# Order of the bf16 and the fp32 products inside the row-tiled fills of a three-layer decoder kernel

## Chip, cores and metric

The kernel runs on one core of one Trainium2 chip. The metric is the device time of one execution in microseconds; for the kernel before it is 3608.37 us, the median of three runs (3608.07 to 3608.52).

## What is computed

The input is x, 64 sequences of 256 tokens with 256 features, and a context of 64 x 120 x 256. Every sequence passes, on its own, through four blocks, each with a layer norm ahead and a residual sum behind:

```python
x = x + local_attention(ln(x))          # 16 heads of 16, each token sees 7 neighbours
x = x + cross_attention(ln(x), ctx)     # 16 heads, 256 queries, 120 keys
x = x + causal_attention(rms(ln(x)))    # 16 heads, 256 queries, 256 keys, mask above the diagonal
x = x + gated_mlp(rms(ln(x)))           # 256 -> 1024 -> 256, weighted by a top-2 gate
```

The change touches only the scores of the cross and the causal attention. They are computed twice. A first time (step "max") with the queries on the partitions, to find each query's maximum m over the keys of each head; a second time (step "scores") with the keys on the partitions, to form exp(scale * (k.q - m)), which is then multiplied with the values.

## The kernel before

**Steps and order.** A planner (class Plan) simulates the engines with written costs and writes out one fixed order of steps for each engine; five sequences are in flight at a time, so neighbouring steps on TensorE mostly belong to different sequences. A step of TensorE waits on semaphores for its operands and for PSUM banks to be emptied, issues its products, and signals the banks as filled (`filled[b]`); ScalarE or VectorE read the bank and signal `emptied[b]`. The costs of the planner are not touched by the change, so the order of steps on every engine stays.

**Row-tiled fills.** A head has 16 features, and two heads share 32 partitions, so the products of "max" (line 756) and "scores" (line 788) contract over 32 rows only. They use the array as four row groups, r = 0 to 3 (`tile_position=(32 * r, 0)`), each writing its own PSUM bank: a fill takes four banks at once. Four products, one in each row group, run beside one another; they are called a quad here. Each fp32 product of the source is two instructions on the chip, each with a weight load of its own; a bf16 product is one. All other steps (projections, transposes, MLP, values) use the array in another shape.

**What is added in bf16.** In the causal "max" fills the mask is added by small bf16 products, `pick_rows` times `mask_rows` (line 750), that add -1e30 above the diagonal. In all "scores" fills the negated maxima are added by `pick` times `nmaxT` (line 780). Before the change these stand first in their fill, with `start=True` on the first of a bank, and the fp32 products accumulate on top. Cross "max" fills have no bf16 part.

**Fills of one sequence,** with quads as instructions on the chip:

| fill | bf16 quads (columns) | fp32 quads (columns) |
|---|---|---|
| cross max, two of them | none | 8 (120) |
| cross scores, two | 2 (256), weights 32x120 | 4 (256) |
| causal max, block 0 | 4 (128) | 8 (128) |
| causal max, block 1, two | 4 (64) | 4 (256) |
| causal scores, units 0 and 1 | 2 (256) | 4 (256) |
| causal scores, unit 2 | 4 (128) | 8 (128) |

**Order around them.** In the trace the steps of TensorE come back in one cyclic order, about 55 us a round, and the ten fills stand in six groups: (a) behind transposes (680): causal scores unit 2, then cross max, then a projection (722); (b) behind that projection: cross max, then causal max block 0, then transposes (687); (c) behind transposes: cross scores, then a projection (700); (d) behind a projection (839): cross scores, then a causal max of block 1, then 700; (e) behind transposes: the other causal max of block 1, then the values (811); (f) behind an MLP product (860): causal scores unit 0, then unit 1, then the MLP's second product (869). Causal scores unit 1 needs a bank that VectorE empties at line 1355.

Of the kernel before, what the change touches and what calls it, by code (L numbers as in the profile page):

```python
# [7 lines left out]
P = 128  # L8
# [10 lines left out]
SLOT = 32  # L19
# [15 lines left out]
LOCAL, CROSS, CAUSAL = 0, 1, 2  # L35
# [6 lines left out]
HEADS = [(m, e, r) for m in range(2) for e in range(2) for r in range(4)]  # L42
# [9 lines left out]
def key_blocks(layer, T, C):  # L52

    if layer == CROSS:
        return [(0, C, 0, T, 0)]
    return [(0, P, 0, T, 0), (P, P, P, P, T)]
# [344 lines left out]
def decoder(nc, t, out):  # L401
    B, T, D = t["x"].shape
    C = t["ctx_1024"].shape[1]
# [6 lines left out]
    with ExitStack() as ctx:  # L410
# [6 lines left out]
        ps = ctx.enter_context(nc.psum_tensor("ps", [P, 8, 512], F32))  # L417
# [15 lines left out]
        pick = sb("pick", [P, 4, P], BF16)  # L433
# [8 lines left out]
        pick_rows = sb("pick_rows", [P, 4, P], BF16)  # L442
# [9 lines left out]
        qT = [[held[s][:, 2 + 2 * e:4 + 2 * e, :] for e in range(2)] for s in range(LANES)]  # L452
        kT = [held[s][:, 6:8, :] for s in range(LANES)]
# [16 lines left out]
        nmaxT = per_lane("nmaxT", [P, T], BF16)  # L470
# [8 lines left out]
        ms = per_lane("ms", [P, 2])  # L479
# [33 lines left out]
        filled = [sem(f"filled{b}") for b in range(BANKS)]  # L513
# [57 lines left out]
        with nc.Block(no_gpsimd_drain=True) as block:  # L571
# [71 lines left out]
            def _(pe):  # L643
# [15 lines left out]
                for name, seq, args in plan.order["PE"]:  # L659
                    s = plan.lane[seq]  # L660
                    once(pe, known, "constants", constants, 16)
                    if name == "derive":

                        b = bank(name, seq, (0,))
                        for slab in range(4):
                            last = nc.tensor.matmul(ps[:, b, slab * P:(slab + 1) * P], like_rows[:, slab, :],
                                                    ident_b[:], start=(slab == 0), stop=(slab == 3),
                                                    skip_group_check=True)
# [3 lines left out]
                                         stop=True).then_inc(filled[b], 1)  # L672
                    elif name == "turn":
# [3 lines left out]
                        for k in range(2):  # L677
                            for tb in range(2):
                                col = k * T + tb * P
                                last = nc.tensor.transpose(ps[:, b, col:col + P], xn[s][:, tb, k * P:(k + 1) * P],  # L680
                                                           ident[:])
                        last.then_inc(filled[b], 1)
                    elif name == "turn_ctx":
                        pe.wait_ge(ctx_loaded[s], reached["ctx_loaded", "load", seq, ()])
                        b = bank(name, seq, args)
                        for k in range(2):
                            last = nc.tensor.transpose(ps[:, b, k * C:(k + 1) * C], cx[s][0:C, k * P:(k + 1) * P],
                                                       ident[0:C, 0:C])
                        last.then_inc(filled[b], 1)
                    elif name == "project_rows":  # L690
                        w, = args
                        n = 1 if w == "q" else 0
# [3 lines left out]
                        for tb in range(2):  # L696
                            for k in range(2):

                                tokens = xT[s][:, k, :].rearrange("p (t b) -> p b t", b=2)[:, tb, :]
                                last = nc.tensor.matmul(ps[:, b, tb * D:(tb + 1) * D], tokens,  # L700
                                                        W[f"local_{w}"][:, k, :], start=(k == 0), stop=(k == 1))
                        last.then_inc(filled[b], 1)
                    elif name == "project":
                        L, w = args
# [6 lines left out]
                        if L == CROSS and w != "q":  # L711
                            wait_taken(pe, "turn_ctx", seq)
                            src, n = cT[s], C
                        else:
                            wait_taken(pe, "turn", seq, L)
                            src, n = xT[s], T
                        b = bank(name, seq, args)
                        wt = W[f"{NAMES[L]}_{w}"]
                        if w in "qk":
                            for m in range(2):  # L720
                                for k in range(2):
                                    last = nc.tensor.matmul(ps[:, b, m * n:(m + 1) * n], wt[:, k, m * P:(m + 1) * P],  # L722
                                                            src[:, k, 0:n], start=(k == 0), stop=(k == 1))
                        else:
                            for tb in range((n + P - 1) // P):
                                rows = min(P, n - tb * P)
                                for k in range(2):
                                    last = nc.tensor.matmul(ps[0:rows, b, tb * D:(tb + 1) * D],  # L728
                                                            src[:, k, tb * P:tb * P + rows], wt[:, k, :],
                                                            start=(k == 0), stop=(k == 1))  # L730
                        last.then_inc(filled[b], 1)
                    elif name == "max":
                        L, f = args
                        tb, ms, keys = max_fills(L, T, C)[f]
# [5 lines left out]
                            wait_taken(pe, "project", seq, L, w)  # L740
                        to = banks(name, seq, args)
                        count = 2 * len(ms)
                        if L == CAUSAL:

                            for slab in range(4):
                                for r in range(4):
                                    rows = slice(32 * r, 32 * r + 32)
                                    of_heads = ps[:, to[r], 0:count * keys].rearrange("p (g k) -> p g k", k=keys)
                                    first = tb * P + SLOT * slab
                                    nc.tensor.matmul(of_heads[:, :, first:first + SLOT], pick_rows[rows, slab, :],  # L750
                                                     mask_rows[rows, :].unsqueeze(1).to_broadcast([32, count, SLOT]),
                                                     start=(slab == 0), stop=False, tile_position=(32 * r, 0),
                                                     skip_group_check=True)
                        for n, (m, e, r) in enumerate((m, e, r) for m, e, r in HEADS if m in ms):
                            rows, place = slice(32 * r, 32 * r + 32), n // 4
                            last = nc.tensor.matmul(ps[:, to[r], place * keys:(place + 1) * keys],  # L756
                                                    qT[s][e][rows, m, tb * P:(tb + 1) * P], kT[s][rows, m, 0:keys],
                                                    start=(L == CROSS and place == 0), stop=True,
                                                    tile_position=(32 * r, 0), skip_group_check=True)
                            if place == count - 1:  # L760
                                last.then_inc(filled[to[r]], 1)
                    elif name == "shift":
                        L, = args
                        pe.wait_ge(nmax_ready[s], reached["nmax_ready", "round_max", seq, (L,)])
                        b = bank(name, seq, args)
                        to = ps[:, b, :].bitcast(BF16)
                        for tb in range(2):
                            last = nc.tensor.transpose(to[:, tb * P:(tb + 1) * P], nmax_parts[s][:, tb, :],
                                                       ident_b[:])
                        last.then_inc(filled[b], 1)  # L770
                    elif name == "scores":
                        L, u = args
                        once(pe, known, "pick", derived["pick"], 1)
                        wait_taken(pe, "shift", seq, L)
                        to, unit = banks(name, seq, args), score_units(L)[u]
                        for n, (g, kb) in enumerate(unit):
                            key0, keys, q0, qs, col = key_blocks(L, T, C)[kb]
                            for r in range(4):
                                rows = slice(32 * r, 32 * r + 32)
                                nc.tensor.matmul(ps[0:keys, to[r], n * qs:(n + 1) * qs], pick[rows, g, 0:keys],  # L780
                                                 nmaxT[s][rows, q0:q0 + qs], start=(n == 0), stop=False,
                                                 tile_position=(32 * r, 0), skip_group_check=True)
                        for n, (g, kb) in enumerate(unit):
                            m, e = divmod(g, 2)
                            key0, keys, q0, qs, col = key_blocks(L, T, C)[kb]
                            for r in range(4):
                                rows = slice(32 * r, 32 * r + 32)
                                last = nc.tensor.matmul(ps[0:keys, to[r], n * qs:(n + 1) * qs],  # L788
                                                        kT[s][rows, m, key0:key0 + keys],
                                                        qT[s][e][rows, m, q0:q0 + qs], start=False, stop=True,  # L790
                                                        tile_position=(32 * r, 0), skip_group_check=True)
                                if n == len(unit) - 1:
                                    last.then_inc(filled[to[r]], 1)
                    elif name == "values":
                        L, = args
# [7 lines left out]
                        for m in range(2):  # L803
                            b = bank(name, seq, (L, m))
                            for e in range(2):
                                g = 2 * m + e
                                pr = prob_of(seq, L, g)
                                for kb, (key0, keys, q0, qs, col) in enumerate(blocks):
                                    for j in range(4):
                                        head = VW * (8 * m + 2 * j + e)  # L810
                                        last = nc.tensor.matmul(ps[SLOT * j:SLOT * (j + 1), b, e * T + q0:e * T + q0 + qs],  # L811
                                                                va[s][0:keys, kb, head:head + SLOT],
                                                                pr[0:keys, j, col:col + qs],
                                                                start=(e == 0 and kb == 0),
                                                                stop=(kb == len(blocks) - 1),
                                                                tile_position=(0, SLOT * j), skip_group_check=True)
                            last.then_inc(filled[b], 1)
                    elif name == "turn_out":
# [3 lines left out]
                        for k in range(2):  # L822
                            for tb in range(2):
                                col = k * T + tb * P
# [3 lines left out]
                    elif name == "project_out":  # L828
                        L, = args
# [13 lines left out]
                    elif name == "gate":  # L843
# [3 lines left out]
                        for tb in range(2):  # L847
                            for k in range(2):
                                last = nc.tensor.matmul(ps[:, b, tb * E:(tb + 1) * E],  # L849
                                                        xT[s][:, k, tb * P:(tb + 1) * P], w_gate[:, k, :],  # L850
                                                        start=(k == 0), stop=(k == 1))
# [557 lines left out]
```

## Time and profile before

| | |
|---|---|
| median of three runs | 3608.37 us |
| the profiled execution: its own time | 3603.33 us |
| its span, first to last instruction | 3601.5 us |
| PE busy | 3488.3 us, 97% |
| PEld (weight loads) busy | 2853.8 us, 79% |
| DVE, POOL, ACT busy | 77%, 70%, 48% |
| PE's share of the chain that ended last | 93% |

PE is the row of matrix products, PEld that of the weight loads of the same engine, which overlap it. A timeline row gives the start of a block of equal instructions in us from the start of the span, the length of the block from its first start to its last end, and how many instructions were merged; a product's recorded end is later than the end of its stream of columns by a constant, so the lengths of two blocks of one shape are compared, or starts with starts.

### The profile page before, as it was taken

What the parts mean: (1) busy time and instruction counts of PE and PEld (TensorE: products, weight loads), DVE (VectorE), ACT (ScalarE), POOL (GpSimd) and SP (SyncE); (2) the same over time, 40 slices, a digit from 0 to 9 for tenths busy, and PEclk for the clock granted to TensorE, in tenths of its full rate; (3) what the DMA queues carried; (4) which work ended last, traced back from release to release, by engine and by line L of the source; (5) the groups of instructions that cost most, each with busy time, mean ns of one, the idle gap of its engine ahead of it and who ended that gap; (6) DMA issues with size and microseconds to landing.
All of it is one profiled execution on the core that took longest, in us unless ns stands there. A gap on an engine that the chain in (4) does not pass through costs nothing.

```text
span 3601.5 us, 97036 instructions
## 1 busy us (share of the span) xinstructions
PE 3488.3 (97%) x38789; PEld 2853.8 (79%) x38789; DVE 2764.0 (77%) x6256; ACT 1715.7 (48%) x4049; POOL 2507.6 (70%) x3159
## 2 busy tenths in 40 slices
PE   6699999999999999999999999999999999999998
PEld 5578888888888888888888888888888888888876
DVE  5677787787787787787787877877877877877863
ACT  2345545545545445445545545445445455455443
POOL 5767777777777677677677777777677677677742
PEclk8899999999999999999999999999999999999999
DMA  5111111111121121121121121111111111111100
GB/s 177 48 50 59 61 67 53 66 69 48 67 72 45 67 74 45 67 74 45 67 74 45 67 73 46 67 67 53 67 63 57 67 60 60 67 57 62 67 8 10
DMA packets 87098, 221.54 MB, mean 62 GB/s; under 512 B 8262, under 2 KB 53634, under 8 KB 70274
## 3 DMA queue, kind: packets, MB, share of 16 engines
q1 hardware_dynamic: 86658, 215.34, 16.9%
q8 instruction: 317, 5.19, 0.6%
q14 instruction: 123, 1.01, 0.1%
HBM read 164.92 MB, written 50.39 MB: 60 GB/s over the span
## 4 chain that ended last, share of the span: by engine, by line
PE 93%; DVE 4%; ACT 2%; issue 1%; POOL 0%; DMA 0%; SPq 0%; DVEq 0%; ACTq 0%
PE ps L869 13%; PE ps L860 13%; PE ps L722 11%; PE ps L700 10%; PE ps L839 9%; PE ps L756 8%; PE ps L811 8%; PE ps L788 6%; PE ps L728 5%; PE ps L680 3%; PE ps L780 3%; PE ps L849 2%; DVE held L1355 1%; PE ps L750 1%; ACT rest L1002 1%; DVE nmax_pair L1292 1%
## 5 line engine op out<-in xcount | busy, mean ns | idle before, releaser
L1124 POOL TENSOR_TENSOR chunks<-v_windows,xT 128x560 f32<-128x560 f32 (+1 forms) x384 | 870.8, 2284 | 259.0 <-DVE xT L1267 155.0
L1292 DVE TENSOR_REDUCE nmax_pair<-ps 128x4 f32<-128x480 f32 (+2 forms) x1280 | 776.1, 669 | 167.8 <-PE ps L756 167.5
L1119 POOL TENSOR_TENSOR chunks<-rest,k_windows 128x512 f32<-128x512 f32 (+1 forms) x384 | 552.9, 1455 | 436.8 <-DVE xT L1246 232.6
L969 ACT ACTIVATE prob<-ps 128x256 f32<-128x256 f32 (+2 forms) x1536 | 670.0, 548 | 331.9 <-PE ps L788 331.9
L860 PE MATMUL ps<-xT,w_up 128*128 128x256 f32 x2048 | 483.7, 384 | 0.0
L869 PE MATMUL ps<-w_down,held 128*128 128x256 f32 x2048 | 458.9, 382 | 1.8 <-DVE held L1355 1.6
L869 PEld LDWEIGHTS ps<-w_down,held 128*128 128x128 f32 x2048 | 383.9, 190 | 72.2 <-issue 20.4
L860 PEld LDWEIGHTS ps<-xT,w_up 128*128 128x128 f32 x2048 | 375.7, 191 | 44.7 <-issue 0.9
L1246 DVE TENSOR_REDUCE xT<-chunks 128x32 f32<-128x512 f32 (+1 forms) x384 | 294.0, 766 | 128.0 <-POOL chunks L1119 128.0
L927 ACT COPY xT<-ps 128x512 f32<-128x512 f32 x256 | 149.8, 585 | 489.3 <-PE ps L680 489.2
L1136 POOL TENSOR_SCALAR_AFFINE_SELECT prob<-prob 128x512 f32<-128x512 f32 x512 | 319.5, 655 | 75.7 <-ACT prob L969 75.7
L756 PE MATMUL ps<-held 32*128 32x256 f32 (+2 forms) x8192 | 358.9, 307 | 3.4 <-ACT held L944 3.3
L788 PE MATMUL ps<-held 32*120 32x256 f32 (+2 forms) x6144 | 341.7, 345 | 0.0
L811 PE MATMUL ps<-prob,va 120*32 120x256 f32 (+2 forms) x6144 | 304.8, 346 | 3.3 <-ACT prob L969 2.4
L756 PEld LDWEIGHTS ps<-held 32*128 32x128 f32 x8192 | 280.2, 187 | 30.4 <-ACT held L940 19.6
L1246 DVE TENSOR_REDUCE held<-chunks 128x80 f32<-128x560 f32 (+1 forms) x384 | 286.8, 760 | 11.6 <-POOL chunks L1124 11.5
L1355 DVE SCALAR_TENSOR_TENSOR held<-rest,ps 128x512 f32<-128x512 f32 x256 | 175.2, 685 | 120.6 <-ACT rest L1002 120.5
L811 PEld LDWEIGHTS ps<-prob,va 120*32 120x32 f32 (+1 forms) x6144 | 180.2, 110 | 108.2 <-issue 25.8
L1002 ACT ACTIVATE rest<-ps 128x512 f32<-128x512 f32 x256 | 152.6, 597 | 224.4 <-PE ps L860 224.4
L788 PEld LDWEIGHTS ps<-held 32*120 32x120 f32 (+1 forms) x6144 | 244.5, 185 | 11.3
L915 ACT ACTIVATE held<-x,nmean,rstd 128x256 f32<-128x256 f32 x256 | 139.9, 594 | 236.5 <-POOL nmean L1072 236.5
L944 ACT ACTIVATE held<-ps,b_cross_q,half 128x256 f32<-128x256 f32 x256 | 123.5, 562 | 109.3 <-PE ps L722 109.3
(146 smaller groups left out, 6086.6 us busy)
## 6 DMA issues: line engine op xcount, KB each, us to landing
k_windows<-passed_on SPq DMA_DIRECT2D x64, 1024.0 KB, 4.6
v_windows<-passed_on SPq DMA_DIRECT2D x64, 1024.0 KB, 5.1
x<-in_x SPq DMA_DIRECT2D x64, 256.0 KB, 2.9
passed_on<-rest SPq DMA_DIRECT2D x64, 256.0 KB, 2.0
passed_on<-held SPq DMA_DIRECT2D x64, 256.0 KB, 2.0
out<-x SPq DMA_DIRECT2D x64, 256.0 KB, 2.1
y<-in_ctx SPq DMA_DIRECT2D x64, 120.0 KB, 2.8
w_up<-in_up SPq DMA_DIRECT2D x1, 1024.0 KB, 8.8
```

The lines of the kernel that those rows point to most:

```text
L700: last = nc.tensor.matmul(ps[:, b, tb * D:(tb + 1) * D], tokens, W[f"local_{w}"][:, k, :], start=(k == 0), stop=(k == 1))
L722: last = nc.tensor.matmul(ps[:, b, m * n:(m + 1) * n], wt[:, k, m * P:(m + 1) * P], src[:, k, 0:n], start=(k == 0), stop=(k == 1))
L756: last = nc.tensor.matmul(ps[:, to[r], place * keys:(place + 1) * keys], qT[s][e][rows, m, tb * P:(tb + 1) * P], kT[s][rows, m, 0:keys], s ...
L788: last = nc.tensor.matmul(ps[0:keys, to[r], n * qs:(n + 1) * qs], kT[s][rows, m, key0:key0 + keys], qT[s][e][rows, m, q0:q0 + qs], start=F ...
L811: last = nc.tensor.matmul(ps[SLOT * j:SLOT * (j + 1), b, e * T + q0:e * T + q0 + qs], va[s][0:keys, kb, head:head + SLOT], pr[0:keys, j, c ...
L860: last = nc.tensor.matmul(ps[:, b, m * T:(m + 1) * T], w_up[:, k, (2 * m2 + m) * P:(2 * m2 + m + 1) * P], xT[s][:, k, :], start=(k == 0), ...
L869: last = nc.tensor.matmul(ps[:, b, tb * D:(tb + 1) * D], hid[s][:, m, tb * P:(tb + 1) * P], w_down[:, m, :], start=(m == 0), stop=(m == F ...
L969: last = nc.scalar.activation(prob_pair(seq, L, m)[0:keys, :, r, col:col + qs], of_pair, ACT.Exp, scale=SCALE)
L1119: last = nc.gpsimd.tensor_tensor(chunk_of(c).rearrange("p (j d) -> p j d", d=D), q_row, window("k", (b + first) * D, (D, n), (1, D)), ALU. ...
L1124: last = nc.gpsimd.tensor_tensor(chunk_of(c).rearrange("p (h i j) -> p h i j", i=HD, j=WINDOW), window("v", b * D + first * HD, (HD, n), ( ...
L1246: nc.vector.tensor_reduce(to, chunk_of(c).rearrange("p (x i) -> p x i", i=width), AX_X, ALU.add).then_inc(reduced[s], 1)
L1292: nc.vector.tensor_reduce(nmax[s][:, tb, heads], src, AX_X, ALU.max, negate=True).then_inc(emptied[b], 1)
```

## The change

In both kinds of step the bf16 products move behind the fp32 ones. The fp32 product that comes first in a bank now has `start=True`; the last bf16 product of a bank now signals `filled`. Nothing is added or removed, and waits stand where they stood, at the head of the step.

```diff
@@ step "max"
                         count = 2 * len(ms)
+                        for n, (m, e, r) in enumerate((m, e, r) for m, e, r in HEADS if m in ms):
+                            rows, place = slice(32 * r, 32 * r + 32), n // 4
+                            last = nc.tensor.matmul(ps[:, to[r], place * keys:(place + 1) * keys],
+                                                    qT[s][e][rows, m, tb * P:(tb + 1) * P], kT[s][rows, m, 0:keys],
+                                                    start=(place == 0), stop=(L == CROSS),
+                                                    tile_position=(32 * r, 0), skip_group_check=True)
+                            if L == CROSS and place == count - 1:
+                                last.then_inc(filled[to[r]], 1)
                         if L == CAUSAL:
...
-                                    nc.tensor.matmul(of_heads[:, :, first:first + SLOT], pick_rows[rows, slab, :],
+                                    last = nc.tensor.matmul(of_heads[:, :, first:first + SLOT], pick_rows[rows, slab, :],
                                                      mask_rows[rows, :].unsqueeze(1).to_broadcast([32, count, SLOT]),
-                                                     start=(slab == 0), stop=False, tile_position=(32 * r, 0),
+                                                     start=False, stop=(slab == 3), tile_position=(32 * r, 0),
                                                      skip_group_check=True)
-                        for n, (m, e, r) in enumerate((m, e, r) for m, e, r in HEADS if m in ms):
-                            rows, place = slice(32 * r, 32 * r + 32), n // 4
...
+                                    if slab == 3:
+                                        last.then_inc(filled[to[r]], 1)
@@ step "scores"
                         for n, (g, kb) in enumerate(unit):
-                            key0, keys, q0, qs, col = key_blocks(L, T, C)[kb]
-                            for r in range(4):
-                                rows = slice(32 * r, 32 * r + 32)
-                                nc.tensor.matmul(ps[0:keys, to[r], n * qs:(n + 1) * qs], pick[rows, g, 0:keys],
-                                                 nmaxT[s][rows, q0:q0 + qs], start=(n == 0), stop=False,
-                                                 tile_position=(32 * r, 0), skip_group_check=True)
-                        for n, (g, kb) in enumerate(unit):
                             m, e = divmod(g, 2)
...
                                                         kT[s][rows, m, key0:key0 + keys],
-                                                        qT[s][e][rows, m, q0:q0 + qs], start=False, stop=True,
+                                                        qT[s][e][rows, m, q0:q0 + qs], start=(n == 0), stop=False,
                                                         tile_position=(32 * r, 0), skip_group_check=True)
+                        for n, (g, kb) in enumerate(unit):
+                            key0, keys, q0, qs, col = key_blocks(L, T, C)[kb]
+                            for r in range(4):
+                                rows = slice(32 * r, 32 * r + 32)
+                                last = nc.tensor.matmul(ps[0:keys, to[r], n * qs:(n + 1) * qs], pick[rows, g, 0:keys],
+                                                 nmaxT[s][rows, q0:q0 + qs], start=False, stop=True,
+                                                 tile_position=(32 * r, 0), skip_group_check=True)
                                 if n == len(unit) - 1:
                                     last.then_inc(filled[to[r]], 1)
```

## Rows read from the trace of the kernel before

**Rows 1.** The page: busy time of each engine, and the chain that ended last
```profile
PE 3488.3 (97%) x38789; PEld 2853.8 (79%) x38789; DVE 2764.0 (77%) x6256; ACT 1715.7 (48%) x4049; POOL 2507.6 (70%) x3159
...
PE 93%; DVE 4%; ACT 2%; issue 1%; POOL 0%; DMA 0%; SPq 0%; DVEq 0%; ACTq 0%
```
**Rows 2.** Waits of PE: who was waited for, total us, times, longest
```profile
PE ps L780 <- DVE held L1355: 22.5, 60, 0.4
PE ps L825 <- DVE held L1246: 16.1, 2, 15.4
```
**Rows 3.** Groups of PE by form: busy us, mean ns of one
```profile
L756 PE MATMUL ps<-held 32*128 32x120 f32 x4096 | 143.8, 278 | 3.4 <-ACT held L944 3.3
L756 PE MATMUL ps<-held 32*128 32x256 f32 x2048 | 142.8, 395 | 0.0
...
L788 PE MATMUL ps<-held 32*128 32x256 f32 x2048 | 134.5, 378 | 0.0
...
L780 PE MATMUL ps<-nmaxT,pick 32*128 32x128 bf16 x1024 | 25.7, 217 | 2.6 <-ACT prob L969 2.6
```
**Rows 4.** Timeline of PE, 1802 to 1811 us: start, length, count (groups a, b)
```profile
1802.82 0.40 PE L780 MATMUL ps<-nmaxT,pick 32*128 32x128 bf16 x16
1803.05 1.12 PE L788 MATMUL ps<-held 32*128 32x128 f32 x32
1804.00 1.05 PE L756 MATMUL ps<-held 32*128 32x120 f32 x32
...
1808.64 1.17 PE L756 MATMUL ps<-held 32*128 32x120 f32 x32
1809.69 0.40 PE L750 MATMUL ps<-mask_rows,pick_rows 32*128 32x128 bf16 x16
1809.91 1.13 PE L756 MATMUL ps<-held 32*128 32x128 f32 x32
```
**Rows 5.** Weight loads (PEld): three forms of the whole trace, mean ns, then one timeline row
```profile
L788 PEld LDWEIGHTS ps<-held 32*128 32x128 f32 x4096 | 155.2, 187 | 4.0
...
L780 PEld LDWEIGHTS ps<-nmaxT,pick 32*128 32x128 bf16 x2048 | 32.2, 92 | 81.8 <-issue 78.6 <-DVE nmaxT L1306 1.7 <-ACT prob L969 1.2
L780 PEld LDWEIGHTS ps<-nmaxT,pick 32*120 32x120 bf16 x1024 | 25.2, 129 | 39.1 <-issue 33.7 <-DVE nmaxT L1306 4.5 <-ACT prob L969 0.7
...
1809.66 0.26 PEld L750 LDWEIGHTS ps<-mask_rows,pick_rows 32*128 32x128 bf16 x16
```
**Rows 6.** Timeline of PE, 1818 to 1825 us (groups c, d)
```profile
1818.27 0.43 PE L780 MATMUL ps<-nmaxT,pick 32*120 32x256 bf16 x8
1818.54 1.03 PE L788 MATMUL ps<-held 32*120 32x256 f32 x16
...
1823.42 1.03 PE L788 MATMUL ps<-held 32*120 32x256 f32 x16
1824.29 0.28 PE L750 MATMUL ps<-mask_rows,pick_rows 32*128 32x64 bf16 x16
1824.40 1.11 PE L756 MATMUL ps<-held 32*128 32x256 f32 x16
```
**Rows 7.** Timeline of PE, 1831 to 1833 us (group e)
```profile
1831.84 1.11 PE L756 MATMUL ps<-held 32*128 32x256 f32 x16
1832.89 0.42 PE L811 MATMUL ps<-prob,va 120*32 120x256 f32 x4
```
**Rows 8.** Timeline of PE, 1846 to 1850 us (group f)
```profile
1846.81 0.40 PE L780 MATMUL ps<-nmaxT,pick 32*128 32x256 bf16 x8
...
1848.45 0.40 PE L780 MATMUL ps<-nmaxT,pick 32*128 32x256 bf16 x8 [0.38 <-DVE held L1355]
1848.67 1.05 PE L788 MATMUL ps<-held 32*128 32x256 f32 x16
```
**Rows 9.** Timeline of PE, 1814.7 to 1815 us: another change of shape
```profile
1814.74 0.28 PE L768 MATMUL ps<-ident_b,nmax_parts 128*128 128x128 bf16 x2
1814.95 1.29 PE L811 MATMUL ps<-prob,va 128*32 128x256 f32 x24
```

More of the change, by code:

```diff
@@ L749, in _ @@
                                     first = tb * P + SLOT * slab
-                                    nc.tensor.matmul(of_heads[:, :, first:first + SLOT], pick_rows[rows, slab, :],
+                                    last = nc.tensor.matmul(of_heads[:, :, first:first + SLOT], pick_rows[rows, slab, :],
                                                      mask_rows[rows, :].unsqueeze(1).to_broadcast([32, count, SLOT]),
-                                                     start=(slab == 0), stop=False, tile_position=(32 * r, 0),
+                                                     start=False, stop=(slab == 3), tile_position=(32 * r, 0),
                                                      skip_group_check=True)
-                        for n, (m, e, r) in enumerate((m, e, r) for m, e, r in HEADS if m in ms):
-                            rows, place = slice(32 * r, 32 * r + 32), n // 4
-                            last = nc.tensor.matmul(ps[:, to[r], place * keys:(place + 1) * keys],
-                                                    qT[s][e][rows, m, tb * P:(tb + 1) * P], kT[s][rows, m, 0:keys],
-                                                    start=(L == CROSS and place == 0), stop=True,
-                                                    tile_position=(32 * r, 0), skip_group_check=True)
-                            if place == count - 1:
-                                last.then_inc(filled[to[r]], 1)
+                                    if slab == 3:
+                                        last.then_inc(filled[to[r]], 1)
                     elif name == "shift":
@@ L776, in _ @@
                         for n, (g, kb) in enumerate(unit):
-                            key0, keys, q0, qs, col = key_blocks(L, T, C)[kb]
-                            for r in range(4):
-                                rows = slice(32 * r, 32 * r + 32)
-                                nc.tensor.matmul(ps[0:keys, to[r], n * qs:(n + 1) * qs], pick[rows, g, 0:keys],
-                                                 nmaxT[s][rows, q0:q0 + qs], start=(n == 0), stop=False,
-                                                 tile_position=(32 * r, 0), skip_group_check=True)
-                        for n, (g, kb) in enumerate(unit):
                             m, e = divmod(g, 2)
@@ L787, in _ @@
                                 rows = slice(32 * r, 32 * r + 32)
-                                last = nc.tensor.matmul(ps[0:keys, to[r], n * qs:(n + 1) * qs],
+                                nc.tensor.matmul(ps[0:keys, to[r], n * qs:(n + 1) * qs],
                                                         kT[s][rows, m, key0:key0 + keys],
-                                                        qT[s][e][rows, m, q0:q0 + qs], start=False, stop=True,
+                                                        qT[s][e][rows, m, q0:q0 + qs], start=(n == 0), stop=False,
                                                         tile_position=(32 * r, 0), skip_group_check=True)
+                        for n, (g, kb) in enumerate(unit):
[5 more added lines that the diff above has]
+                                                 tile_position=(32 * r, 0), skip_group_check=True)
                                 if n == len(unit) - 1:
```

## The prediction

> **What bounds the kernel now.** I read the page first: PE is busy 97% of the span and holds 93% of the chain that ended last, with ScalarE and VectorE at a few per cent [rows 1]. Then the waits of PE: one wait comes back in every round, 60 times for 22.5 us in all, that of the second of two causal score fills for a bank that VectorE empties; the next is 16.1 us in only two occurrences [rows 2]. So a nanosecond that PE gains or loses inside a fill goes into the end time, save where that one wait follows. The rest is how PE's own stream is fitted together, and for that the timelines of one round are read, block by block [rows 4 to 8].
>
> **The pace inside a fill.** Four row groups run beside one another, so I count quads. An fp32 quad of 128 columns takes 0.11 us: the cross max at 1804.00, 8 quads, lasts 1.05 us; less the length of one product, 0.278, that is 7 x 0.11 [rows 3, 4]. A quad of 256 columns takes 0.216: 1.03 us for four, less 0.378 [rows 3, 6], over three. The bf16 ones take half of that or less: 0.056 for 128 columns (four quads in 0.23 us from 1802.82 to 1803.05, 0.01 of it a head [rows 4]), 0.029 for 64 (0.11 to 0.12 for four [rows 6]), 0.108 for 256 (half of the fp32 quad). These streams stay; only what lies between them changes.
>
> **Two kinds of loss.** A *head* is the first weight load after the array changes shape. The cross max at 1808.64 comes behind a projection and lasts 1.17 us; its twin at 1804.00, behind another row-tiled fill, lasts 1.05 [rows 4]. So a first load in fp32 costs 0.12 us. A first load in bf16 costs 0.02 to 0.03 (the block at 1802.82 lasts 0.40, against 3 x 0.056 and a length of 0.217 [rows 3, 4]), and 0.05 to 0.06 with 120 columns (0.27 from 1818.27 to 1818.54, less 2 x 0.108 [rows 6]). That fits the records of the loads: 187 ns in fp32, 92 in bf16, 129 in bf16 with 120 columns [rows 5].
>
> A *seam* is the place where fp32 follows bf16: the fp32 load is longer than the bf16 quad it should hide under. Causal max of block 1 lasts 1.11 us against 1.03 for the same four fp32 quads behind longer bf16 ones [rows 6]: 0.08 us. Over the whole trace its products have a mean of 395 ns against 378, 17 ns more; in 4 of 16 instructions that is 0.07 to 0.08 [rows 3]. Behind 128-column bf16 quads it is 0.05 to 0.06: from 1803.05 to 1804.00 are 0.95 us for 8 x 0.11 [rows 4]. Behind 256-column ones it is under 0.01 (1.03 us is already the bare length). The opposite seam, bf16 behind fp32, costs nothing: from 1823.42 to 1824.29 is 0.87 us for 4 x 0.216 [rows 6], since a 92 ns load hides under any fp32 quad. Only at 1809.66 does a bf16 load start late, about 0.02 after the fp32 stream before it had ended (1808.64 + 1.17 - 0.16 = 1809.65), with its first product at 1809.69 [rows 4, 5]; the semaphore waits of the step stand between, and they stay.
>
> **The sum, for one round (us, a plus is slower).** The change turns every seam around, so the seams within a fill vanish, and it turns every bf16 head into an fp32 one.
> - Heads behind another shape: causal scores unit 2 (group a) +0.09, cross scores (c) and (d) +0.05 each (0.12 less 0.055, and a 120-column fp32 load is a little shorter), causal max of block 1 (e) +0.09. Together +0.28.
> - Heads within a run, where the first load starts late. Causal max block 0 (b): late as just read, +0.08. Causal scores unit 1 (f): it starts when VectorE lets it (1848.45, idle 0.38 [rows 8]), so nothing covers its load, +0.08. For both the bounds are 0 and 0.12; I take the value near the fp32 head, as their load begins when the array is already idle or about to be.
> - Causal scores unit 0 (f): +0.09, but it stands ahead of that 0.38 us wait, whose end is set by the MLP product before, by ScalarE and by VectorE: counted as 0. If this cover were gone it would be +0.09.
> - Seams removed: two of 0.055 (scores unit 2, max block 0), two of 0.08 (max of block 1), four of under 0.01: -0.28.
> - Seam added: the cross max of group (a) now follows bf16 quads of 128 columns instead of fp32 ones, with 128-column fp32 weights: +0.055, bounds 0 and 0.08. Max of block 1 in (d) follows 256-column quads: 0.
> - Leaving the row-tiled shape costs the same behind either type. At 1831.84 the fp32 block has its seam of 0.08 and four quads, to 1832.79, and the next load is at 1832.89; two bf16 products from 1814.74 end their streams at 1814.86, and the next starts at 1814.95 [rows 7, 9]: 0.09 to 0.10 in both. 0.
> - Signals: a bank's `filled` goes out with its last product. Its length beyond the stream is 378 - 216 = 0.16 us in fp32, and 0.217 - 0.056 = 0.16 in bf16 [rows 3]: 0 for ScalarE and VectorE. No DMA, no step of POOL, SP or another queue moves, and no wait is added; the waits at the head of a step hold the same instructions behind them.
> - bf16 products that accumulate onto a bank are not in the trace. The nearest rows are fp32: quads that accumulate onto bf16 ones take 0.216 as others do, so 0; the other bound is in the rivals.
>
> 0.28 + 0.16 - 0.28 + 0.055 = +0.21 us a round, over 64 rounds (62 in the steady part) +13 us. The profiled execution took 3603.3 us around a span of 3601.5, 5 us or 0.14% under the median; I put the sum on the median: 3621 us.
>
> **Rule against row.** By the rows, a first load behind a change of shape is exposed, and in fp32 that is 0.12 us. The Trainium skill ("TensorE: Matmul & The Clock Gate", part 2) says that TensorE pulls a weight load ahead of products in flight into a background buffer; by that alone heads would cost nothing. "TensorEngine Tiling (Array Packing)", Key Properties, says that changing the tiling mode drains the engine; by that they are exposed, and the trace agrees with this one (0.12 us against 0). The same first page also says that fast weight load holds for 128 weights in a type other than fp32; the trace agrees, 92 ns against 129 for 120 weights.
>
> **Rivals.**
> - *Heads stay hidden (faster).* If fp32 heads cost what bf16 heads do, only the seams are left: -0.28 + 0.055 = -0.23 a round, -14 us, 3594. It decides in favour of the change once an fp32 head costs under 0.05 us more than a bf16 one. The pull-ahead rule of the skill named above would give this. Against it stands the 1.17 against 1.05 [rows 4]. Chance 0.07.
> - *Partly absorbed.* The late heads (+0.16) hide in full under waits that stand there anyway, or later steps catch up on a release that is as late as before: +0.05 a round, 3 us, 3612 with what remains. For it: max block 0 starts late already. Against: its bf16 products start right behind their load. Chance 0.14.
> - *Waits lose their cover (slower still).* The sequencer works through a step's semaphore waits while queued products run. With short bf16 quads at the end, less time is queued; the start at 1809.66 shows that this can show. At the two seams within runs (a, d), 0.1 each: +0.2 a round, 3634. Against: the fp32 quads ahead of them are queued too. Chance 0.08.
> - *Accumulating bf16 products are slower.* Bf16 streams of a round are six of 0.22 us and two of 0.12, 1.56 in all. Twice as slow, and without the hidden one of causal scores unit 0, that is +1.3 us a round, 85 us, 3706 with the forecast. No row suggests it. Chance 0.02.
> - *The change does nothing*, because the instructions are issued in another order than the source's: the rows show them in the order of the source. Within 0.01.
>
> **Numbers.** The forecast case has 0.69, with its own range 3615 to 3629. A measurement of this kernel can tell 0.2%, 7.2 us, from no change. Faster: the first rival, 0.07. Same: the absorbed case and the low edge of the forecast, 0.14. Slower: 0.79. The range of 3612 to 3632 takes in the forecast's unknowns (late heads 0 to 0.12 each, +/-5 us; the added seam +/-3) and most of the absorbed case, and leaves out 2 in 10.
>
> **What would show it.** The block of causal scores unit 2 should start with fp32, last 0.12 longer than bare, and carry no seam; max of block 1 should last 0.08 less from end to end; the cross max behind bf16 should show a long first quad; weight loads at the heads should be fp32 behind the same idle time; PE's wait for line 1355 should shrink by some 5 us. It would be wrong if an fp32 head shows as short as a bf16 one, if bf16 quads pace slower than 0.056, or if new repeated waits appear in PE's list.

## The result and the profile after

The changed kernel takes 3628.82 us (median of four runs, 3626.72 to 3633.44) against 3608.22 us for the kernel before (median of four, 3600.97 to 3608.52): a ratio of 1.0062, 95% interval 1.0050 to 1.0074. A second measurement on another occasion gave 1.0062, 1.0049 to 1.0075. So it is slower by 0.6%, 21 to 22 us. The forecast was 13 us more, 3621 us, with a range of 3612 to 3632 us. Two executions of the experiments below, one of the version with only causal max fill 1 changed (7060 us) and one of that with only the cross scores changed (12473 us), are slow runs without a trace and are left out of the medians.

The page of the changed kernel, first the engines, then its chain that ended last [against rows 1]:

```profile
PE 3524.1 (97%) x38789; PEld 2926.2 (81%) x38789; DVE 2769.6 (76%) x6256; ACT 1717.5 (47%) x4049; POOL 2512.7 (69%) x3159
...
PE 91%; DVE 4%; ACT 2%; DMA 2%; POOL 1%; issue 1%; DVEq 0%; POOLq 0%; ACTq 0%; SPq 0%
```

PE is still the bound. It holds the same 38789 products and is busy 36 us longer in a span 30 us longer; the 6 us between are the wait that shrinks in the next view. PE's waits [against rows 2]; line 1357 is line 1355 of before:

```profile
PE ps L783 <- DVE held L1357: 16.6, 60, 0.3
...
PE ps L851 <- DVE nmax_pair L1294: 3.4, 5, 0.9
```

The wait that came back in every round has lost 5.9 us, 0.10 in each of 60. The second row is new; it is read below.

**One round, group by group.** Timeline of PE in the changed kernel (start us, length us, count), in the same round as rows 4 to 8 of the kernel before. The fp32 score products are line 783 now and their bf16 products 791; the fp32 maxima are 745, the mask 758:

```profile
1817.71 0.60 PE L680 MATMUL ps<-ident,held 128*128 128x128 f32 x4
1818.24 1.17 PE L783 MATMUL ps<-held 32*128 32x128 f32 x32
1819.23 0.40 PE L791 MATMUL ps<-nmaxT,pick 32*128 32x128 bf16 x16
1819.46 1.12 PE L745 MATMUL ps<-held 32*128 32x120 f32 x32
1820.50 1.99 PE L722 MATMUL ps<-xT,w_causal_q 128*128 128x256 f32 x8
1822.34 1.89 PE L722 MATMUL ps<-xT,w_causal_k 128*128 128x256 f32 x8
1824.15 2.23 PE L745 MATMUL ps<-held 32*128 32x120 f32 x64
1826.17 0.43 PE L758 MATMUL ps<-mask_rows,pick_rows 32*128 32x128 bf16 x16
1826.54 0.42 PE L687 MATMUL ps<-ident,y 120*128 120x120 f32 x2
...
1833.22 0.66 PE L680 MATMUL ps<-ident,held 128*128 128x128 f32 x4
1833.81 1.14 PE L783 MATMUL ps<-held 32*120 32x256 f32 x16
...
1835.10 2.00 PE L700 MATMUL ps<-w_local_k,xT 128*128 128x256 f32 x8
1836.93 1.89 PE L841 MATMUL ps<-w_causal_o,xT 128*128 128x256 f32 x8
...
1839.93 1.04 PE L745 MATMUL ps<-held 32*128 32x256 f32 x16
1840.80 0.29 PE L758 MATMUL ps<-mask_rows,pick_rows 32*128 32x64 bf16 x16
1841.03 2.00 PE L700 MATMUL ps<-w_local_v,xT 128*128 128x256 f32 x8
...
1846.76 0.60 PE L680 MATMUL ps<-ident,held 128*128 128x128 f32 x4
...
1848.48 1.93 PE L813 MATMUL ps<-prob,va 120*32 120x256 f32 x32
...
1858.80 3.67 PE L862 MATMUL ps<-xT,w_up 128*128 128x256 f32 x16
1862.41 1.15 PE L783 MATMUL ps<-held 32*128 32x256 f32 x16
...
1864.05 1.15 PE L783 MATMUL ps<-held 32*128 32x256 f32 x16 [0.28 <-DVE held L1357]
...
1865.34 5.01 PE L871 MATMUL ps<-w_down,held 128*128 128x256 f32 x22
```

The steps that frame the groups in the kernel before, in the same view (the others are in rows 4, 6, 7 and 8):

```profile
1802.29 0.60 PE L680 MATMUL ps<-ident,held 128*128 128x128 f32 x4
...
1805.00 1.98 PE L722 MATMUL ps<-xT,w_causal_q 128*128 128x256 f32 x8
1806.82 1.89 PE L722 MATMUL ps<-xT,w_causal_k 128*128 128x256 f32 x8
...
1810.97 0.42 PE L687 MATMUL ps<-ident,y 120*128 120x120 f32 x2
...
1817.69 0.66 PE L680 MATMUL ps<-ident,held 128*128 128x128 f32 x4
...
1819.50 2.00 PE L700 MATMUL ps<-w_local_k,xT 128*128 128x256 f32 x8
1821.34 1.89 PE L839 MATMUL ps<-w_causal_o,xT 128*128 128x256 f32 x8
...
1825.45 2.00 PE L700 MATMUL ps<-w_local_v,xT 128*128 128x256 f32 x8
```

and for the groups (e) and (f) of before:

```profile
1831.18 0.60 PE L680 MATMUL ps<-ident,held 128*128 128x128 f32 x4
...
1843.21 3.67 PE L860 MATMUL ps<-xT,w_up 128*128 128x256 f32 x16
...
1849.65 0.70 PE L869 MATMUL ps<-w_down,held 128*128 128x256 f32 x2
```

From the start of the step ahead of a group to the start of the step behind it (us, rows round to 0.01). The last column, in ns, tells for each fill of the group how much later it ends than before, beyond what the step ahead of it was already late: the median over the rounds between 300 and 3300 us.

| group | before | after | difference | each fill, median (ns) |
|---|---|---|---|---|
| (a) scores unit 2, cross max | 2.71 | 2.79 | +0.08 | +45 +53 |
| (b) cross max, causal max block 0 | 4.15 | 4.20 | +0.05 | +46 |
| (c) cross scores | 1.81 | 1.88 | +0.07 | +60 |
| (d) cross scores, causal max fill 1 | 4.11 | 4.10 | -0.01 | +60 -81 |
| (e) causal max fill 2 | 1.71 | 1.72 | +0.01 | +19 |
| (f) causal scores units 0 and 1 | 6.44 | 6.54 | +0.10 | +99 +0 |

A projection behind (b) takes back 0.02, since it waited on VectorE by that much before. The medians add up to +0.28 us. The whole rounds say the same. The MLP's second product (line 869, now 871), two occurrences 20 rounds apart, before and after:

```profile
1632.13 7.17 PE L869 MATMUL ps<-w_down,held 128*128 128x256 f32 x32
...
2719.64 7.17 PE L869 MATMUL ps<-w_down,held 128*128 128x256 f32 x32
```

and of the changed kernel:

```profile
1646.70 7.17 PE L871 MATMUL ps<-w_down,held 128*128 128x256 f32 x32
...
2739.90 7.17 PE L871 MATMUL ps<-w_down,held 128*128 128x256 f32 x32
```

1087.51 / 20 = 54.375 us a round before, 1093.20 / 20 = 54.660 after: +0.285.

### The profile page after: what moved, and what is told of

The parts are those of the page before. It is cut to its first block, busy times and chain, and to the rows that moved or that the text cites. A ratio compares the mean times of both kernels' runs of the same rounds, so it can differ in the third digit from the quotient of the medians.

```text
span 3631.7 us, 97036 instructions
## 1 busy us (share of the span) xinstructions
PE 3524.1 (97%) x38789; PEld 2926.2 (81%) x38789; DVE 2769.6 (76%) x6256; ACT 1717.5 (47%) x4049; POOL 2512.7 (69%) x3159
## 4 chain that ended last, share of the span: by engine, by line
PE 91%; DVE 4%; ACT 2%; DMA 2%; POOL 1%; issue 1%; DVEq 0%; POOLq 0%; ACTq 0%; SPq 0%
PE ps L862 13%; PE ps L871 13%; PE ps L722 11%; PE ps L700 9%; PE ps L841 9%; PE ps L745 8%; PE ps L813 8%; PE ps L783 8%; PE ps L728 4%; PE ps L680 3%; PE ps L851 2%; PE ps L791 2%; DVE held L1357 1%; ACT rest L1004 1%; DMA k_windows<-passed_on 1%; DVE nmax_pair L1294 1%
## 5 line engine op out<-in xcount | busy, mean ns | idle before, releaser
L783 PE MATMUL ps<-held 32*120 32x256 f32 (+2 forms) x6144 | 373.3, 364 | 26.6 <-DVE held L1357 16.6
```

What stands on the lines that cost most here:

```text
L783: nc.tensor.matmul(ps[0:keys, to[r], n * qs:(n + 1) * qs], kT[s][rows, m, key0:key0 + keys], qT[s][e][rows, m, q0:q0 + qs], start=(n == 0) ...
```

## The experiments

All use one source in which a function tells how many bf16 quads stand ahead of the fp32 products in each fill (all, as before the change; 0, as after it; or 1). Theory H is that of the prediction, heads and seams.

**Score fills alone.**

```diff
+def bf16_first(name, args, quads):
+    return 0 if name == "scores" else quads
```

> Only the score fills have their bf16 products last; the causal max fills keep the mask products first. Theory H (heads and seams, in us a round of 62): two cross score fills +0.06 each, causal scores unit 2 +0.10 head and -0.055 seam, the cross max behind it +0.05, causal scores units 0 and 1 together +0.10: +0.32 a round, +20 us, so about as slow as the full change or a little under it, 3626 to 3630. Rival Q (each bf16 product that comes last and accumulates onto a bank costs something of its own, wherever it stands): cost goes by the number of bf16 quads moved, 12 of 24 here, so half of the full change's 21 us, +10 us. Rival S (the loss is in the start and the tail of the run, not in the rounds): anything between 0 and 20, with no change of the block lengths in the steady part.

Measured: 3628.54 us against 3609.08, ratio 1.0058, 1.0045 to 1.0071, +19 to 21 us. A round grows by 0.32 us at the median (by fills: unit 0 +99 ns, cross scores +60 twice, cross max behind unit 2 +53, unit 2 +45). As H says; Q's +10 us lies below the interval.

**Causal max fills alone.**

```diff
+def bf16_first(name, args, quads):
+    return 0 if name == "max" else quads
```

> Only the causal max fills have their mask products last; the score fills are as before. Theory H: block 0 +0.10 head -0.055 seam -0.02 that a later wait takes up, the block-1 fill behind cross scores -0.08 (its head hides under 256-column quads), the one behind transposes +0.10 -0.08: -0.04 a round, -2 us, 3604 to 3608: same. Rival Q: 12 of 24 bf16 quads are moved: +10 us, 3618.

Measured: 3610.34 against 3609.08, ratio 1.0005, 0.9996 to 1.0013: no difference that can be told. The medians of a round are block 0 +45 ns, fill 1 -83, fill 2 +18, and -20 behind: -0.04 us, as H says. Moving 12 of the 24 bf16 quads behind costs nothing of its own, and Q falls.

**One bf16 quad first, the others last.** This is the run that takes the heads away and leaves bf16 products at the end.

```diff
+def bf16_first(name, args, quads):
+    return min(1, quads)
```

> In each fill one bf16 quad stands first, then all fp32 quads, then the other bf16 quads. Theory H: every head is a bf16 head again and every fill has its seam back, so all is as before but for the cross max that follows 128-column bf16 quads, +0.05 a round: +3 us, 3610 to 3613. Rival Q: 16 of 24 bf16 quads stand last and accumulate: +14 us, 3622.

Measured: 3613.38 against 3609.08, ratio 1.0010, 1.0001 to 1.0019, +4 us; Q's +14 us lies above the interval. The group (a) in this kernel's timeline of PE (lines 797 bf16 and 811 fp32 are the scores, 768 the maxima):

```profile
1807.49 0.23 PE L797 MATMUL ps<-nmaxT,pick 32*128 32x128 bf16 x4
1807.56 1.12 PE L811 MATMUL ps<-held 32*128 32x128 f32 x32
1808.50 0.34 PE L797 MATMUL ps<-nmaxT,pick 32*128 32x128 bf16 x12
1808.67 1.11 PE L768 MATMUL ps<-held 32*128 32x120 f32 x32
```

One bf16 quad is enough for a bf16 head; the seam behind it is back (1.12 us for the fp32 block, as before), and the cross max now stands behind bf16 quads and has grown from 1.05 to 1.11 us, the added seam. Over the rounds only this one changed, +53 ns; all others are within 7 ns of before. The change's loss is its heads.

**Causal max fill 1 alone.** It stands behind a cross score fill, inside a row-tiled run, in 56 rounds of the steady part.

```diff
+def bf16_first(name, args, quads):
+    return 0 if (name, args) == ("max", (CAUSAL, 1)) else quads
```

> Only causal max fill 1 (block 1, first half of the heads), which stands behind a cross score fill in nearly every round, has its mask products last. Theory H: its fp32 head hides under the 256-column quad ahead of it and its seam of 0.08 goes: -0.08 a round, -5 us, 3603, faster than both kernels. Rival Q: +3 us, 3611. If a head inside a run were exposed too: +0.02 a round, 3609.

Measured: 3600.96 against 3609.08 (seven runs), ratio 0.9977, 0.9966 to 0.9987: faster than both kernels. Its timeline (line 811 is the cross scores' fp32 part, 768 the maxima, 756 the mask):

```profile
1821.65 1.03 PE L811 MATMUL ps<-held 32*120 32x256 f32 x16
1822.52 1.03 PE L768 MATMUL ps<-held 32*128 32x256 f32 x16
1823.38 0.28 PE L756 MATMUL ps<-mask_rows,pick_rows 32*128 32x64 bf16 x16
```

The maxima start 0.87 us after the scores, which is 4 x 0.216, so the head is hidden; they last 1.03 us where before it was 1.11 [rows 6], so the seam is gone: -83 ns a round. The kernel was run a second time:

> The version with only causal max fill 1 changed once more: theory H has -0.08 us a round, -5 us, ratio 0.9986; the first measurement had 0.9977. If that was luck in the tail, the ratio now comes out at 0.998 to 1.000.

Measured: 3602.85 against 3607.15, ratio 0.9991, 0.9983 to 1.0000. Both intervals hold the 0.9986 that the 5 us of the rounds account for, the first only just; the second reaches 1.0000, so that the whole times alone would be thin evidence. Its profile has -83 ns in each round again.

**Cross scores alone: the head by itself.**

```diff
+def bf16_first(name, args, quads):
+    return 0 if (name, args[0]) == ("scores", CROSS) else quads
```

> Only the two cross score fills have their bf16 products last. They have no seam to lose (256-column bf16 quads), so this is the head alone. Theory H: +0.06 each, +0.12 a round, +7.4 us, 3616, and the blocks show a first quad that starts 0.06 later behind its load. Rival Q (a price for each bf16 quad that comes last): the one-quad-first run left little room for it, under 0.1 us a round, so under +4 us here.

Measured: 3617.05 against 3607.15 (seven runs), ratio 1.0031, 1.0020 to 1.0042, +10 to 11 us, with +60 ns in each of the two fills in every round and nothing elsewhere: 7.4 us from the rounds. The expected +7.4 us is at the lower edge of the interval; some 3 us are not in the rounds (see the start and the tail, below). One sign was expected wrongly: the first quad is recorded where it was before, and it is the second that comes late, 0.31 us behind the first in fp32 against 0.16 in bf16, where the streams differ by 0.11.

**Unit 0 of the causal scores alone: is its head covered?**

```diff
+def bf16_first(name, args, quads):
+    return 0 if (name, args) == ("scores", (CAUSAL, 0)) else quads
```

> Only causal scores unit 0 has its bf16 products last. Theory H: its head costs 0.10 us, and PE's wait for the bank that VectorE empties, just behind it, shrinks from 22.5 us in all to about 17: nothing left in a round, a total within the spread of before (3600 to 3612). Rival: the bank's release is itself late when unit 0 is late (through ScalarE's queue), then +0.10 a round, +6 us, and the wait stays at 22 us.

Measured: 3603.64 us, one run. PE's waits in this kernel:

```profile
PE ps L797 <- DVE held L1380: 16.5, 60, 0.3
```

Unit 0 is 99 ns later in every round and unit 1 takes back 99: the wait shrinks from 22.5 to 16.5 us [rows 2]. The cover holds.

**Unit 1 alone: is a first load taken ahead while PE waits?**

```diff
+def bf16_first(name, args, quads):
+    return 0 if (name, args) == ("scores", (CAUSAL, 1)) else quads
```

> Only causal scores unit 1 has its bf16 products last. It starts when the bank is released, so nothing covers its first load. Theory H: +0.10 us a round in full, +6 us, and the wait stays at 22.5 us. Rival: the fp32 load is taken ahead while PE waits, then 0 a round.

Measured: 3614.30 us, one run beside one of before at 3608.40. PE's waits, then the weight loads and the products of unit 1 in one round:

```profile
PE ps L811 <- DVE held L1380: 22.5, 60, 0.4
...
1851.92 0.77 PEld L811 LDWEIGHTS ps<-held 32*128 32x128 f32 x16 [0.75 <-issue]
...
1851.95 1.15 PE L811 MATMUL ps<-held 32*128 32x256 f32 x16 [0.37 <-DVE held L1380]
```

The wait is whole, and unit 1 takes 98 ns more in every round. The first load starts at 1851.92, with the product and not ahead of it: nothing of it is done in the 0.4 us of waiting.

**Both kernels again: what is not in the rounds.**

> The changed kernel once more, for a narrower ratio and a second profile. If the rounds carry the loss: +0.28 us in each steady round again, 17 us, and a ratio near 1.0055. If start, tail and late window fetches carry part of it: their share differs from the first profile's (4.9 us up to the end of the first sequence, 4.7 us in the tail, 3 us in five rounds), while the rounds' share stays.

> The kernel before once more, one look. If the tail, the start and the rounds whose window fetch lands late vary by themselves, this profile differs from the first by some us in just those places, and its steady rounds are the same to 0.01 us. If the first profile of before was typical, the tail has its one half-clock stretch again and 3 late fetches.

> The changed kernel a third time. Up to the end of the first sequence its two profiles stood 4.9 and 5.0 us behind the first one of before, and two profiles of before differed by 0.5 there; one of the other kernels stood at -6.9. If the change makes the start slower, about +5 again; if it is chance, anything from -7 to +7. The rounds: +0.28 each.

> The kernel before a third time, beside it: its start within 1 us of its other two if the start is typical of a kernel, or off by some us if it is chance; the rounds the same to 0.01 us; the tail between 0 and +6 us of the first profile.

Ratio of the changed kernel 1.0062, 1.0049 to 1.0075 (3631.35 against 3607.15). Single runs gave 3610.14 and 3611.57 for before and 3625.39 for after. From the timelines, in us, cut at the start of the MLP's second product of the first sequence and at that of the sequence numbered 57 (three profiles each):

| | up to the first | 57 rounds | from there to the end of the span |
|---|---|---|---|
| before | 218.6, 218.0, 220.2 | 3099.2, 3100.3, 3099.9 | 283.7, 290.1, 289.8 |
| after | 223.4, 223.6, 218.9 | 3118.9, 3116.2, 3117.1 | 289.4, 291.3, 287.5 |
| means' difference | +3.1 | +17.6 | +1.6 |

The middle is certain: +17.6 us in 57 rounds. Of this 57 x 0.28 = 16 us are in every round; the rest is mostly a wait of the gate step for VectorE in a few rounds (3.4 us in 5 rounds, 1.1 in 2 and 1.9 in 4 in the three profiles after). In the first of these rounds of the first profile VectorE is late because its reduction waits for GpSimd, whose first window product waits for the fetch of the k rows. That fetch is late in 9, 7 and 9 rounds after, and in 3, 7 and 3 before, by GpSimd's waits for it; whether the change makes it so is open. Start and tail scatter by 5 to 8 us between profiles of one kernel (with only fill 1 changed, the first sequence's second product ends at 226 us in one profile and at 219 in the other), so their +3 and +2 are not shown to be the change's. The profile of before that the prediction used had the shortest tail of the three.

What start and tail scatter with can be read from the granted clock, the number behind the busy times in these windows (start and end of the window; length; busy us and count of PE, PEld, DVE, ACT, POOL; granted clock; DMA share; GB/s), for the first profile of before:

```profile
120.00:180.00 60.00, 45.49 (x580) 35.41 (x583) 42.15 (x89) 23.39 (x52) 40.52 (x39) 0.85 0.15 54
180.00:240.00 60.00, 53.90 (x608) 42.74 (x612) 43.92 (x99) 25.57 (x62) 40.11 (x49) 0.91 0.09 30
```

and for the first profile after:

```profile
120.00:180.00 60.00, 47.50 (x540) 37.82 (x544) 38.59 (x81) 25.89 (x56) 40.31 (x43) 0.80 0.16 54
180.00:240.00 60.00, 53.94 (x589) 42.84 (x582) 42.46 (x94) 24.38 (x58) 39.74 (x46) 0.86 0.09 30
```

Between 300 and 3300 us it is 1.00, the level of 2.4 GHz, in all fourteen profiles. In the start (it is lowest between 60 and 120 us, 0.64, where PE is busy for 28 of the 60 us) it is at the half level, 1.2 GHz, for 75 us in each of the three profiles of before and for 85, 85 and 79 us in those after; over all kernels, the shortest start (212 us) has 61 us of it and the longest (226 us, the cross scores alone) 89. In the tail the half level holds for 6, 17 and 20 us before and 17, 16 and 13 us after, in the order of the table, and the only two tails of 284 us are the two with 6 us. So start and tail are longer where more of them ran at the lower level. Whether the lower level makes them longer or comes from the same waits, and whether the change has a part in it, is not shown.

## Why the prediction was right, and where it was off

- **What bounds.** PE, in the rounds: 17.6 of the 22 us by which the mean spans of three profiles differ are there, and each change inside a fill reached the end time, but for unit 0.
- **Heads.** Right in kind and in place; this is the term that was too small. I took 0.09 for an fp32 head instead of a bf16 one, 0.05 with 120 columns, and 0.08 for the two late ones. The single-fill runs have 0.10, 0.06 and 0.10 (unit 1; block 0 gave 0.045, which is 0.10 less the seam of 0.055). Together 0.01 + 0.01 + 0.01 + 0.01 + 0.02 + 0.02 = 0.08 us a round. The value had been read from a block of 120-column products against one of the same shape, with the difference 0.12 less 0.03 on rows of 0.01, and rounded down further (0.065 to 0.05 with 120 columns, 0.09 to 0.08 for the late ones). The lengths of the load records, which stood beside it, come close to what was measured: 187 less 92 is 95 ns, and with 120 columns 183 (the fp32 score loads of the whole trace) less 129 is 54.
- **Seams.** Removed ones 0.083 (fill 1 alone) and 0.055 (by the rows, and by the 0.045 that unit 2 and block 0 are left with), the added one 0.053, 256-column ones nothing: as forecast. Bf16 behind fp32 costs nothing, as forecast (from 1839.93 to the bf16 block at 1840.80 is 0.87 us, 4 x 0.216).
- **Unit 0.** Hidden, as forecast; the wait lost 5.9 us where I had 5.
- **Leaving the row-tiled shape, signals, accumulating bf16 products.** No cost: group (e) is +19 ns, which is a head of 0.10 less a seam of 0.083, and in the run with one quad first, where fills also end in bf16, every step keeps to 7 ns of before, but for the added seam.
- **A small give-back.** The 20 ns that the step behind (b) takes back were not in the sum.
- **The sum.** +0.21 forecast, +0.28 found; 13 us forecast, 16 us in the steady rounds. The remaining 4 to 6 us (the fetch, the start, the tail) were in no step of the prediction, and their cause is not settled. That the measured time lies in the range all the same, 3 us under its upper end, is in part luck: the range was made for the late heads and the added seam.
- **Rivals.** Heads do not stay hidden (cross scores alone, 60 ns each; unit 1 alone, 98 ns); beyond unit 0, nothing was absorbed but 20 ns; the semaphore waits behind bf16 quads cost nothing more (the cross max behind them grew by its seam alone); accumulating products are not slower.
- **Block 0.** Its head of 0.10 stood inside a row-tiled run, behind a cross max, while the first loads of fill 1 behind the cross scores and of the cross max behind unit 2 are hidden. The prediction had this from the late load at 1809.66 and put it on the semaphore waits between. That part stays open: ScalarE's last copy ahead of this load had ended at 1809.32, 0.3 us before it, and no run moved these waits.
- **The rule.** By the run of unit 1 a first load is not begun while PE waits for its semaphore. By the group table it is not begun under the products of another array shape either: in (c), (d) and (e) the head is paid behind transposes and behind projections alike. The Trainium skill's rule on pulling loads ahead ("TensorE: Matmul & The Clock Gate", part 2) holds here only within one shape; its sentence on the drain ("TensorEngine Tiling (Array Packing)", Key Properties) agrees with the trace.

## What to carry to other kernels

Where products with short weight loads and products with long ones share a fill on a bound TensorE, begin with the short load wherever the array changes shape or the step starts from a wait: here that is worth 0.10 us each time, 0.06 with 120 columns. Inside a run without such a break begin with the long load, which hides under the product ahead, and put the short products last: worth 0.08 us here with products of 64 columns, 0.055 with 128 and nothing with 256. The version that does only this, in one fill, is faster than both kernels (ratios 0.9977 and 0.9991). Look first whether the load in such a run starts on time: that of causal max block 0 did not, and its head was paid. The kernel with one order in all fills, bf16 first or last, is slower than the one that decides by what stands ahead of the fill in the order of the engine.

## What the runs showed that was not expected

One quad in front is enough: a head costs by the type of the very first load alone. An idle array is no help: with 0.4 us of waiting ahead of it, a first fp32 load was still paid in full, 98 ns more than a bf16 one. And this kernel's time scatters by some 13 us (3600 to 3613 for before), in the profiles mostly in its first 220 and last 290 us and with the granted clock there, while all but two of the 57 rounds of two profiles of before repeat to 0.01 us; step by step, two profiles told a difference of 0.02 us in a round, where whole times needed eleven runs to tell 4 us.
